# Eight clips of rounded weights taken from VectorE to GpSimd in a Mamba, BitNet and attention kernel

## The reference

```
x = x + tanh(g_xattn[0]) * mamba_scan(ctx, gate input = layernorm(x))     # 512 channels, 16 states, 512 steps
x = x + tanh(g_ffn[0])   * bit_ffn(layernorm(x), w1, w2)                  # 512 -> 2048 -> 512, rounded weights
x = x + tanh(g_xattn[1]) * (layernorm(x) @ softmax(q k^T)^T)              # q, k from ctx
x = x + tanh(g_ffn[1])   * ffn(layernorm(x), proj1, proj2)                # 512 -> 2048 -> 512
# in bit_ffn, for w1 and for w2:
rms = rsqrt(max(mean(w * w), eps));  w_quant = clip(round(w * rms), -1, 1) / rms
```

## Time and profile before

| | |
|---|---|
| time, median of 3 runs | 1172.61 us (1170.66 to 1172.63) |
| the profiled execution | 1169.88 us, its span 1168.1 us |
| busy: PE, DVE, ACT, POOL | 828.8, 904.9, 639.3, 563.9 us |
| clips of weights (L1391) | 8 on DVE, mean 1556 ns, from 102.0 to 213 us |

### The profile page before, as it was taken

How to read it: one execution, slowest core, us unless ns; L and a number is a source line. 1 busy time by engine, 2 the same in 40 slices (tenths; PEclk the granted TensorE clock), 3 DMA queues, 4 the chain that set the end, 5 groups by cost and what they waited for, 6 DMA issues and landing times.

```text
span 1168.1 us, 10659 instructions
## 1 busy us (share of the span) xinstructions
PE 828.8 (71%) x2665; PEld 405.5 (35%) x2704; DVE 904.9 (77%) x1151; ACT 639.3 (55%) x889; POOL 563.9 (48%) x462
## 2 busy tenths in 40 slices
PE   5342311298598875899599877889498868887998
PEld 2010100143243332444234333344233323344886
DVE  3889988977888899687888899688878898565333
ACT  5556856467368843275488642365388641432442
POOL 0487568122777665123786674023877673123000
PEclk8565555599789997998799988998699988998999
DMA  7055995000168696220188786300287775200222
GB/s 249 0 106 110 218 260 100 16 1 1 43 139 176 147 228 152 94 86 36 29 173 177 159 199 162 128 0 36 45 179 162 164 185 146 90 1 1 91 91 72
DMA packets 51439, 130.07 MB, mean 111 GB/s; under 512 B 6304, under 2 KB 7456, under 8 KB 50864
## 3 DMA queue, kind: packets, MB, share of 16 engines
q0 software_dynamic: 17280, 62.92, 29.1%
q1 hardware_dynamic: 34096, 66.53, 16.9%
HBM read 62.33 MB, written 4.19 MB: 57 GB/s over the span
## 4 chain that ended last, share of the span: by engine, by line
PE 43%; DVE 22%; issue 12%; POOL 9%; DMA 7%; ACT 6%; POOLq 0%; DVEq 0%; ACTq 0%; SPq 0%; another core or an unknown queue 0%
PE bank L582 12%; DVE pair L1124 7%; PE bank L595 7%; DMA u<-work 6%; POOL work L1508 5%; PE bank L610 4%; PE pair L610 4%; PE pair L526 3%; PE pair L513 2%; PE bank L444 2%; DVE work L1128 2%; PE pair L571 1%; PE bank L452 1%; PE bank L469 1%; DVE u L1135 1%
## 5 line engine op out<-in xcount | busy, mean ns | idle before, releaser
L1124 DVE TENSOR_TENSOR_SCAN pair<-pair,work 128x512 f32<-128x512 f32 x256 | 313.0, 1223 | 49.1 <-ACT pair L797 42.7
L1508 POOL TENSOR_TENSOR work<-du,bcast 128x1024 f32<-128x1024 f32 x128 | 318.3, 2489 | 67.4 <-DMA u<-work 61.8
L797 ACT ACTIVATE pair<-dt,a_neg 128x512 f32<-128x512 f32 x256 | 168.1, 685 | 65.8 <-DVE work L1128 48.4
L582 PE MATMUL bank<-stage,ring 128*128 128x512 f32 x384 | 180.9, 615 | 22.2 <-ACT hx L979 8.0
L1128 DVE TENSOR_TENSOR work<-pair,ccast 128x512 f32<-128x512 f32 x256 | 177.0, 691 | 14.6 <-ACT bcast L782 1.4
L1519 POOL DMA_DIRECT2D u<-work x120 | 113.8, 950 | 81.2 <-DVE work L1128 74.6
L595 PE MATMUL bank<-ring,stage 128*128 128x512 f32 x192 | 94.5, 644 | 41.3 <-DVE stage L1365 39.9
L418 PE MATMUL bank<-xd,pick 128*128 128x512 bf16 x108 | 49.5, 458 | 96.8 <-ACT bcast L782 67.7
L582 PEld LDWEIGHTS bank<-stage,ring 128*128 128x128 f32 x384 | 74.3, 197 | 116.4 <-issue 89.8
L1554 POOL TENSOR_SCALAR stage<-stage,fst 128x2048 f32<-128x2048 f32 x16 | 33.1, 2067 | 119.8 <-DVE fst L1333 119.8
L782 ACT ACTIVATE bcast<-bank 128x512 f32<-128x512 f32 x64 | 38.0, 594 | 76.0 <-POOL work L1508 51.9
(11 more groups left out here) (158 smaller groups left out, 1578.6 us busy)
## 6 DMA issues: line engine op xcount, KB each, us to landing
u<-work POOLq DMA_DIRECT2D x120, 512.0 KB, 5.2
ring<-ffn_dram SPq DMA_DIRECT2D x144, 256.0 KB, 3.6
ring<-ffn_dram SPq DMA_DIRECT2D x16, 512.0 KB, 3.3
xres<-x_dram SPq DMA_DIRECT2D x4, 1024.0 KB, 5.4
stage<-w_dram SPq DMA_DIRECT2D x1, 4096.0 KB, 17.1
stage<-w_dram SPq DMA_DIRECT2D x4, 1024.0 KB, 8.4
out_dram<-stage SPq DMA_DIRECT2D x16, 256.0 KB, 2.8
ctxT<-ctxT_dram SPq DMA_DIRECT2D x4, 512.0 KB, 7.4
```

The source lines that it names most:

```text
L582: last = pe.matmul(banks[2 + f % 2][:], up_slot(f)[:, k * P:(k + 1) * P], xnT[:, k, :], start=k == 0, stop=k == J - 1)
L797: act.activation(pairs[s % DECAYBUFS][:, q, :], dt[:, p * HALF + q, :], ACT.Exp, scale=a_neg[:, p * HALF + q, n:n + 1]).then_inc(s_decay, 1)
L1124: dve.tensor_tensor_scan(state, state, row, 0.0, ALU.mult, ALU.add).then_inc(s_scan, 1)
L1508: pool.tensor_tensor(work[:, s % SCANBUFS, :, :], du[:, p * HALF:(p + 1) * HALF, :], bcast[:, n % 2, :].unsqueeze(1).broadcast_to([P, HALF ...
```

## The change

The four `weight_clip` calls of the pieces of w1 and the four of w2 leave DVE and go to POOL. The instruction is the same, with the same semaphores, on another engine. On POOL the two clips of a slot stand behind all products and accumulations of that slot.

```diff
@@ DVE, mixer_last
                 if slot == GATE_SLOT:
                     for p in range(2):
                         js = slice(p * HALF, (p + 1) * HALF)
-                        if prev is None and p:
-                            weights(slot)
                         last_sum(b, p)
@@ DVE
-            def weight_clip(i, c):
-
-                w = stage[:, c * FF:(c + 1) * FF]
-                dve.wait_ge(s_wscaled, 4 * i + c + 1)
-                dve.tensor_scalar(w, w, MAGIC - 1.0, MAGIC + 1.0, ALU.max, ALU.min).then_inc(s_wclip, 1)
-
-            def weights(slot):
-                if slot in W_ROUND:
-                    i, cs = W_ROUND[slot]
-                    for c in cs:
-                        weight_clip(i, c)
@@ DVE, pass_, between half(m, prev, slot, 0, 0) and half(m, prev, slot, 0, 1)
-                    elif slot != GATE_SLOT:
-                        weights(slot)
@@ POOL
+            def weight_clip(i, c):
+
+                w = stage[:, c * FF:(c + 1) * FF]
+                pool.wait_ge(s_wscaled, 4 * i + c + 1)
+                pool.tensor_scalar(w, w, MAGIC - 1.0, MAGIC + 1.0, ALU.max, ALU.min).then_inc(s_wclip, 1)
+
+            def clips(slot):
+                if slot in W_ROUND:
+                    i, cs = W_ROUND[slot]
+                    for c in cs:
+                        weight_clip(i, c)
@@ POOL, pass_
                     if scans:
                         half(m, prev, slot, 1, 0)
                         half(m, prev, slot, 1, 1)
+                        if not rest:
+                            clips(slot)
                         mixer_last(m, slot)
```

## The result

The kernel got slower: 1204.4 us median (1195.62 to 1217.93, 4 runs) against 1172.62 us (1170.66 to 1172.74), a ratio of 1.025, 95% interval 1.0195 to 1.0305. The ratio is formed without the execution of 1217.93 us, which lies 1.1% above the next one. The forecast was 1176.8 us with a range up to 1181.5. The sign was right, the size was not.

The account below looks back on a forecast made before the run. Only the first pass could move, paced by DVE, then accumulations, then DVE again; the steady loop was untouched. 0 + 3.9 + 0.3 = +4.2 us on 1172.61 gave 1176.8 us, range 1171.5 to 1181.5.

Parts of the forecast that it names:

- the price of a clip on POOL: Each moved clip was taken to cost 2.07 us, from POOL's rounding of the same shape.
- the upper bound of 5.0: Highest price of a clip on POOL, 5.0 us for 2048 elements, from its product with two inputs.
- The rival of dear clips: Clips at 5.0 us each on POOL add 5.9 us in each of slots 7 and 8, 11.7 at the end; chance 0.06.
- The chain of waits: In slots 7 and 8, DVE waits for ACT's decays, ACT for POOL's clips, POOL for its own product.
- Slot 7: First pass: clips leaving DVE become a 7.2 us wait for ACT's decays before step 15; net 0.
- Slot 8: First pass: step 19 starts later, as ACT's decays wait behind POOL's clips; +5.9 us, or +10.2 with a slow accumulation.
- the accumulation of step 16 gets ahead of the second loads: Slot 8: it has the queues for itself and lands in 5.08 us, not 9.41.
- Slots 9 to 11: Part of the delay is caught up, later accumulations get dearer; step 26 and all behind it +3.9 us.
- The late loads: SP's second pair of w2 loads starts some 10 us later, making the accumulations of steps 20 and 22 8.4 us each.
- The end: End of the mixer: 4.6 us of clips leave DVE, but sharing with POOL's four clips eats the gain; +0.3 us.
- by turns: End of the mixer: POOL's four clips and DVE's four last operations alternate in order of arrival, 13.2 us in all.
- What ACT and POOL do after the clips of w2 waits for DVE's next sums anyway: After the clips of w2, at the mixer's end: nothing else moves, so no further cost.

Follow-up runs that it names:

- experiments 1 and 2: experiment 1, then two runs of the changed kernel with eight other instruction forms each at the eight clip places; no time given.
- experiment 1: The changed kernel with POOL's clips replaced by a multiplication by 1 and an addition of 0: 1170.7 us, ratio 1.0001 to the kernel before.
- experiment 3: The kernel before with only the clips of w1 on POOL: 1191.2 us, ratio 1.0156; with only those of w2: 1178.9 us, ratio 1.0071.
- experiment 4: The changed kernel with ACT's quantise of w1 one slot later: 1201.7 us, ratio 1.025 to the kernel before.

## Why the prediction was wrong

**The step that failed is the price of a clip on POOL:** "I take 2.07, as inputs, shape and number of operations are the same; only the operations are max and min". It is 7.07, and the upper bound of 5.0 did not hold it either. The rounding whose 2.07 us I took multiplies and adds, which is one of the cheap pairs. I had read an upper bound out of an instruction with two inputs, as if elements were what POOL is slow at; what counts is the pair of operations (experiments 1 and 2). The rival of dear clips, at 5.0 us, gave 1200 and was nearest to the truth, with a chance of 0.06, but in part by luck: with 7.07 its own sum gives 1176.8 + 8 x 5.0 = 1217, as it has all four clips of w2 stand in DVE's way, 20 us at the end, where experiment 3 has 11.1. A price too low and an end too dear met near the measured time. My estimate of 1.8 us, from the 1.03 cycles an element that GPSIMD Engine Reference (the Trainium skill, section 3.1) gives for one or two operations, fits the cheap pairs (1.9 us) and none of the others.

**The chain of waits was right.** Experiment 1 has clips of 1.9 to 2.2 us and tests the rest of the sum:

- Slot 7, forecast 0, a wait of 7.2 us before step 15: step 15 by the positions 0.1 us early, wait 7.02.
- Slot 8, forecast +5.9: +5.3, wait 6.53. That the accumulation of step 16 gets ahead of the second loads held: it lands in 4.6 us (5.08 forecast), and step 19 would have been at +10.2 otherwise.
- Slots 9 to 11, forecast +3.9: +2.3 at step 26. The late loads cost less than I thought: the accumulations of the steps 20 and 22 land in 8.1 and 6.9 us, where I had taken 8.4 for each. The right way, and 1.6 us too large.
- The end, forecast +0.3: from step 30 to the last gate -0.6. But not by turns, as I had said: the first sum waits for all four clips at once. DVE, then POOL, in experiment 1:

```profile
205.09 5.15 DVE L1243 TENSOR_TENSOR u<-u,work 128x1024 f32<-128x1024 f32 x1
```

```profile
201.38 7.78 POOL L1576 TENSOR_SCALAR stage<-stage 128x2048 f32<-128x2048 f32 x4
```

The sum of both queues is the same either way, so the figure survived the wrong reason: that it came out is luck.

In all +1.4 us at the last gate, where I had forecast +4.2. The time of experiment 1 (ratio 0.9966 to 1.0037) can't tell the two apart, nor from no change.

**With 7.07 put into the same steps** the changed kernel comes out: POOL's product ends at 117.4, two clips at 131.7, the quantise at 133.6, decays at 134.5, step 15 at 135.3, +10.0. Once more in slot 8, where no clip leaves DVE's row in exchange: +25.4 at step 19. These are measured times; the prediction's steps with 7.07 in place of 2.07 give 135.3 and 169.4. The second comes so near in part by luck: the accumulation of step 14 landed in 5.0 us and not in 10.23, and that of step 16 then waited for DVE and went out at 144.07, where the steps have 144.5.

**"What ACT and POOL do after the clips of w2 waits for DVE's next sums anyway"** held for clips of 2 us and failed at 7: four clips last until 252.7, and the inverse roots that DVE needs about 243 stand behind them, 10.3 us. A cover that I named without its limit.

## What to carry to other kernels

Before work moves to GpSimd, price the very pair of operations there: the same `tensor_scalar` on 128x2048 took 1.9 us or 7.1 by its pair, and a row of another pair is no bound. Where the engine that takes the work also feeds the engine that gave it, count the work against its own free time between two of its products, not against its mean busy share. And look where VectorE's instruction meets one of GpSimd before moving it to another engine: a clip that met GpSimd's product took 3.91 us and behind the next step 1.22, and that alone brought the loop's start 2.2 us forward, where no version with clips on GpSimd brought it forward at all. When an edit moves one wait, look what else hangs on the moved instruction; in experiment 4 it was a load.

## What the runs showed of the hardware

- GpSimd's `tensor_scalar`, f32, 128x2048: 1.89 to 2.4 us for multiply and add, add and multiply, multiply and multiply; 7.07 to 7.13 for the others tried in slots 7 and 8; 5.4 to 6.2 for a single operation, all at the mixer's end (5.37 for the one whose row overlaps none ahead).
- The slow form shuts out a VectorE sum of two SBUF operands only for part of its time. In the changed kernel the first clip starts at 223.45, and the sum that was waiting beside it ends at 229.04, so it began about 4.4 us into the clip; the gate of 229.08 and the sum of 230.22 ran their usual 1.2 us, the first wholly beside the clip. With two clips on GpSimd the same again: clip at 202.47, sum free about 206.85. The gate of 231.47 (5.39 us) was held up beside the second clip and still ended 1.5 us before it (236.86 and 238.37). VectorE's own clip of one operand was shut out to the end of GpSimd's (9.42 us for two). SBUF — State Buffer of the Trainium skill, Who interferes with whom, says of VectorE's two-port modes that whoever issues first has the shared ports for the whole instruction and the other blocks fully. For VectorE's clip the trace agrees; VectorE's sums and gate of two SBUF operands were held up for a part only. In experiment 1 four short instructions in a row on GpSimd kept a waiting sum out for 3.9 us, though the last two began after it had started to wait.
- TensorE's clock stood at 1.2 GHz from slot 8 to the loop (in four of the twelve profiles but for one short rise), and when it rose to 2.4 differed: 2.3 us after the first product of the loop (L513) in the kernel before, 5.3 us after it in the changed one, 5.5 us in the run with the clips of slot 7 apart. In the changed kernel (busy time of the engines from 264 to 272 us; the clock, a half of full speed, stands third from the end) the sixteen products from 266.96 took 6.24 us, all but the last 0.9 at the low level:

```profile
264.00:272.00 8.00, 5.74 (x19) 2.26 (x18) 2.32 (x7) 3.85 (x5) 0.00 (x0) 0.50 0.00 0
```

  From the first activation to the first reduction of the loop it took 4.85 us, before 3.37: 1.5 us of its loss. What decides between 2.3 and 5.5 stays open.
- The rest of the span, from the loop's first reduction (L1331, L1329 in the changed kernel) to the end, is the same program in all kernels, and it took 923.9 to 935.1 us in ten profiles, 920.6 and 935.6 in the two of the forms. The time at 1.2 GHz after the rise was 137.5 us in the shortest (920.6), 147.5 in the next two (923.9 and 924.5), 161.2 in one of 931.7 and 174.7 in the longest, so it goes with it closely. What sets the one or the other these runs don't show. This spread of 15 us is of the order of that between executions of the kernel before (1160.7 to 1180.5), and more than most of the edits here are worth. The position of the first activation of the loop judged them better than the time did.
